# One order for three queues: the first stage and the last two pairs of a modulated 4-bit feed-forward kernel

## What is computed

```
gate = relu(cond @ W3 + b3)                                   # 64 x 512, one row per batch
v    = (64 * x + sum of x over the 64 positions) * gate       # x is 64 x 64 x 512
x1   = relu(v @ W2 + b2)                                      # the first stage
w_up = ((w_up_q - 7.5) * scale).T ;  w_down likewise          # 4-bit codes, a scale per 64
x2   = relu(x1 @ w_up + b_up + x1 @ up_a @ up_b)              # 512 -> 2048, low rank 16
out  = x + x2 @ w_down + b_down + x2 @ down_a @ down_b        # 2048 -> 512
```

## Time and profile before

| | us |
|---|---|
| median of 3 runs | 765.02 (764.61 to 765.81) |
| the profiled execution | 765.55 |
| its span in the profile | 763.7 |
| TensorE busy in the span | 740.0 (97%) |
| VectorE, ScalarE, GpSimd busy | 554.5, 420.4, 78.3 |

### The profile page before, as it was taken

How to read it: one execution, slowest core, us unless ns; L and a number is a source line. 1 busy time by engine, 2 the same in 40 slices (tenths; PEclk the granted TensorE clock), 3 DMA queues, 4 the chain that set the end, 5 groups by cost and what they waited for, 6 DMA issues and landing times. The chain is left out here.

```text
span 763.7 us, 9568 instructions
## 1 busy us (share of the span) xinstructions
PE 740.0 (97%) x3248; PEld 609.5 (80%) x3248; DVE 554.5 (73%) x725; ACT 420.4 (55%) x727; POOL 78.3 (10%) x68
## 2 busy tenths in 40 slices
PE   6599999999999999999999999999999999999997
PEld 5478888878878878888888888888888888888876
DVE  6598866776976487767776877767776877757585
ACT  3866175574754175666647265666656363626531
POOL 0063524333430000000000000000000000000000
PEclk9899999999999999999999999999999999999999
DMA  8957978988628696655516798766515696665552
GB/s 325 308 185 218 292 214 264 288 262 250 221 99 290 210 383 230 220 194 193 180 56 229 254 385 265 222 202 192 180 56 183 229 382 220 199 192 194 193 165 111
DMA packets 92160, 170.60 MB, mean 223 GB/s; under 512 B 8528, under 2 KB 25040, under 8 KB 91472
## 3 DMA queue, kind: packets, MB, share of 16 engines
q1 hardware_dynamic: 91824, 169.90, 67.4%
q10 hardware_dynamic: 288, 0.08, 0.0%
HBM read 130.10 MB, written 40.89 MB: 224 GB/s over the span
## 5 line engine op out<-in xcount | busy, mean ns | idle before, releaser
L1138 PE MATMUL ps<-x_hi,ring 128*128 128x512 f32 x672 | 262.1, 390 | 3.0 <-DVE x_lo L932 1.8
L1139 PE MATMUL ps<-x_lo,ring 128*128 128x512 f32 x672 | 261.5, 389 | 0.0
L1140 PE MATMUL ps<-x_hi,ring 128*128 128x512 f32 x672 | 261.4, 389 | 0.0
L1138 PEld LDWEIGHTS ps<-x_hi,ring 128*128 128x128 f32 x672 | 126.1, 188 | 31.4 <-DVE x_lo L932 2.7
L1140 PEld LDWEIGHTS ps<-x_hi,ring 128*128 128x128 f32 x672 | 126.1, 188 | 26.3
L1139 PEld LDWEIGHTS ps<-x_lo,ring 128*128 128x128 f32 x672 | 126.1, 188 | 26.1
L388 ACT ACTIVATE xt<-xt,gated,gate_n 128x64 f32<-128x64 f32 x216 | 74.6, 430 | 37.2 <-DVE gated L741 37.2
L497 ACT ACTIVATE f<-ps,bias 128x512 f32<-128x512 f32 x96 | 64.8, 690 | 42.2 <-PE ps L1140 42.2
L932 DVE TENSOR_TENSOR x_lo<-x_sum,x_hi 128x512 fp32r<-128x512 f32 x96 | 76.8, 818 | 4.2 <-ACT x_hi L535 3.4
L853 DVE TENSOR_TENSOR ps<-s,ps 128x512 f32<-128x512 f32 x48 | 33.3, 693 | 51.1 <-PE ps L1140 50.7
L890 DVE TENSOR_TENSOR res<-ps,res 128x512 f32<-128x512 f32 x72 | 48.3, 687 | 23.6 <-PE ps L1140 23.2
(11 more groups left out here) (80 smaller groups left out, 1002.0 us busy)
## 6 DMA issues: line engine op xcount, KB each, us to landing
ring<-made_w SPq DMA_DIRECT2D x336, 256.0 KB, 3.7
made_w<-made SPq DMA_DIRECT2D x16, 1280.0 KB, 6.0
xt<-in_x SPq DMA_DIRECT2D x32, 256.0 KB, 5.6
code<-in_codes SPq DMA_DIRECT2D x16, 512.0 KB, 8.3
scale<-made_s SPq DMA_DIRECT2D x16, 512.0 KB, 8.0
res<-in_x SPq DMA_DIRECT2D x4, 2048.0 KB, 10.1
made_w<-plain SPq DMA_DIRECT2D x64, 128.0 KB, 6.3
out<-res SPq DMA_DIRECT2D x12, 512.0 KB, 5.5
```

What stands on the lines that cost most here:

```text
L1138: pe.matmul(dest, w_hi, a_hi, start=start, stop=False, skip_group_check=True)
L1139: pe.matmul(dest, w_hi, a_lo, start=False, stop=False, skip_group_check=True)
L1140: return pe.matmul(dest, w_lo, a_hi, start=False, stop=stop, skip_group_check=True)
```

## The change

- TensorE, first stage: chunks 0 to 2 of half 0 run pass by pass (four matmuls high by high, four low weight by high, four high weight by low x), each pass with its own wait, so that the first four need only the high parts. `low_rank(0)` moves from behind tile 4 to behind tile 5.
- Who modulates: DVE tiles 0 and 2, ACT tiles 1, 4 and 7, POOL tiles 3, 5 and 6 (eight instructions of 64 columns each). POOL also rounds `lora` and `wide`; the tables are loaded on 96 of the 128 partitions, in two DMAs.
- Loads: `raw_w3` is sent by output chunk, the first quarter ahead; W2 goes over ACT's queue; the scales of the first two units are copied ahead of the others; x's tiles come in the order 0 to 5, 7, 6.
- DVE's and ACT's lists in the first stage are written in the order in which TensorE takes the tiles.
- Last block: the sums, roundings and subtractions of pairs 6 and 7 alternate, step by step. The very last `tail` is M6 before M7; M6 starts its bank afresh without waiting for a copy, ACT copies BP to `s4` beside it, and DVE adds `s4` to `res`.

The rest of the diff, cut to what is spoken of:

```diff
-    ON_DVE, ON_ACT = (0, 1, 2, 3, 5), (4, 6, 7)
+    ON_DVE, ON_POOL, ON_ACT = (0, 2), (3, 5, 6), (1, 4, 7)
...
             act.dma_start(raw_cond[:], cond[:]).then_inc(cond_loaded, 16)
+            for k in range(KD):
+                act.dma_start(raw_w2[:, k, :], w2[:, k, :]).then_inc(w2_raw[k], 16)
...
+            gate_tile(0)
             w2_high(0)
-            for k in range(KD):
             x_high(0, 0)
-            w2_high(1)
+            for k in range(1, KD):
+                gate_tile(k)
             act.wait_ge(gate_done, KD)
             act.mul(gate_n[:], gate[:], float(SEQ)).then_inc(gate_done, 1)
+            w2_high(1)
+            x_modulate(0, 1)
             x_high(0, 1)
...
+            def x_modulate(t):
+                pool.wait_ge(x_gated, gate_no(0, t))
+                pool.wait_ge(gate_done, KD + 1)
+                for b in range(PER):
+                    part = xt[:, j, k, b * SEQ:(b + 1) * SEQ]
+                    done = pool.tensor_scalar(part, part, gate_n[:, k, batch:batch + 1], gated[:, t, b:b + 1], ALU.mult, ALU.add)
+                done.then_inc(x_mod_pool, 1)
+
+            x_modulate(3)
+            pool.wait_ge(tables_loaded, 16)
+            pool.tensor_copy(lora_flat, raw_lora).then_inc(tab_cast, 1)
+            x_modulate(5)
+            x_modulate(6)
+            pool.tensor_copy(wide_flat[:, 0:T], raw_wide[:, 0:T]).then_inc(tab_cast, 1)
+            pool.wait_ge(rest_loaded, 16)
+            pool.tensor_copy(wide_flat[:, T:], raw_wide[:, T:]).then_inc(tab_cast, 1)
...
             w_tiles:
+                if s == 0 and j == 0 and k < KD - 1:
+                    passes = ((x_hi_done, w2_cast, w2_in_ring[k][:, 0], xm_hi[:, k, :]),
+                              (x_hi_done, w2_split, w2_in_ring[k][:, 1], xm_hi[:, k, :]),
+                              (x_split, w2_split, w2_in_ring[k][:, 0], xt_lo[:, j, k, :]))
...
+                if m == 1:
+                    pe.wait_ge(w3_loaded, 16)
...
-                    if j == 1 and k in (0, KD - 1):
-                        low_rank(k // 3)
+                    if j == 1 and k in (1, KD - 1):
+                        low_rank(k // 2)
...
             behind x_low of tile 7, DVE:
             add_lora(0)
-            x_low(0, 5)
             x1p_low(0, 0)
             x1p_low(0, 2)
-            x_low(0, 6)
+            plain_low(0)
             dequantize(1)
-            x_low(0, 7)
-            plain_low(0)
...
-            wide_low(slice(T, NH * P), 3)
             add_lora(1)
             x1p_low(1, 0)
             x1p_low(1, 2)
+            wide_low(slice(T, NH * P), 3)
...
-            tail(*before)
+            n = len(LAST) - 1
+            wait_bank(pe, BQ, SBS - 1, n)
+            product(SBS - 1, n, M6, BQ, True)
+            pe.wait_ge(q_down_done, down_no(SBS - 1, 3, 1) - 8 + 1)
+            product(SBS - 1, n, M7, BP, False)
```

More of the change, by code:

```diff
@@ L282, in load_scale, with copy_scales @@
                 sp.dma_start(scale[u % 3][:], rows.to_broadcast([2 * COPIES, P // 2 // COPIES, 1024])).then_inc(scale_loaded[u % 3], 16)
+            def copy_scales(units, copied):
+                n = units.stop - units.start
+                sp.dma_start(made_s[units], scales[units].unsqueeze(2).to_broadcast([n, 2, COPIES, 1024])).then_inc(copied, 16)
             def store_plain(u):
@@ L632, in _ @@
                     if n == 13 and last:
-                        x2_high(s, 6, 3)
+                        x2_high(s, 6, 2)
+                        x2_high(s, 7, 2)
+                    if n == 14 and last:
                         x2_high(s, 6, 4)
-                    if n == 14 and last:
-                        x2_high(s, 7, 3)
                         x2_high(s, 7, 4)
@@ L686, in _ @@
                         x2_high(s, (n - 1) // 2, 4)
-                    if n == 12 and last:
-                        x2_high(s, 6, 2)
-                    if n == 13 and last:
-                        x2_high(s, 7, 2)
                     if not last and n in (8, 10):
@@ L1131, in _ @@
             finish_c22(SBS - 1, 1)
+            to = res[:, 3, 1, :]
+            dve.wait_ge(q_down_done, down_no(SBS - 1, 3, 1) - 8 + 1)
+            dve.wait_ge(res_summed, 4 * (SBS - 2) + 4)
+            dve.tensor_tensor(to, to, s4[:], ALU.add).then_inc(res_summed, 1)
+            dve.wait_ge(res_summed, 4 * (SBS - 2) + 5)
+            add_res(*before, BQ)
             add_res(*before, BP)
-            add_res(*before, BQ)
         @block.tensor
@@ L1142, in w_tiles @@
             def w_tiles(s, j, k, bank_of):
+                if s == 0 and j == 0 and k < KD - 1:
+                    passes = ((x_hi_done, w2_cast, w2_in_ring[k][:, 0], xm_hi[:, k, :]),
+                              (x_hi_done, w2_split, w2_in_ring[k][:, 1], xm_hi[:, k, :]),
+                              (x_split, w2_split, w2_in_ring[k][:, 0], xt_lo[:, j, k, :]))
+                    for n, (x_ready, w_ready, still, moving) in enumerate(passes):
+                        pe.wait_ge(x_ready, k + 1)
+                        pe.wait_ge(w_ready, k + 1)
+                        for m in range(KD):
+                            mm = pe.matmul(ps[bank_of(m)][:], still[:, m * P:(m + 1) * P], moving, start=k == 0 and n == 0,
+                                           stop=False, skip_group_check=True)
+                    mm.then_inc(w_step, 1)
+                    return
                 pe.wait_ge(x_split, 8 * s + 4 * j + k + 1)
@@ L1334 @@
         "cond": tiles(a["cond_1024"].T),
-        "w3": tiles(a["cond_W3"]),
+        "w3": tiles(a["cond_W3"]).reshape(P, -1, kd, P).transpose(0, 2, 1, 3),
         "w2": tiles(a["cond_W2"]),
@@ L1339 @@
         "scales": scales,
-        "tables": np.concatenate([by_quadrant(a["ffn_w_up_lora_a"].T, 0), by_quadrant(a["ffn_w_down_lora_b"], rank), wide], 1),
+        "tables": np.concatenate([by_quadrant(a["ffn_w_up_lora_a"].T, 0), by_quadrant(a["ffn_w_down_lora_b"], rank), wide], 1)[:3 * QUAD],
     }
```

170 lines of the change are left out of this document (92 added, 78 removed).

## The result

| | before | after |
|---|---|---|
| median, us | 764.86 (764.61 to 765.81, 4 runs) | 755.45 (754.59 to 755.87, 4 runs) |
| span of the profiled execution | 763.7 | 753.9 |
| ratio | | 0.987, 95% interval 0.9856 to 0.989 |

The change takes 9.4 us off. I had forecast 748.7, 16.3 off, in a range of 744.5 to 756.0: the sign and the range hold, but the likeliest time was 6.8 too low, and 755.45 lies outside the 745 to 752 that I gave the forecast itself. The rest of this document is about those 6.8 us.

What follows compares the result with a forecast made beforehand. TensorE's pace bounds the kernel, with removable waits only in the first stage and last block. Gains of 13.5 - 0.5 + 3.3 = 16.3 us off the median 765.02 give 748.7; 8-in-10 range 744.5 to 756.

Steps and rivals of the forecast that it cites:

- POOL's price: First stage: each POOL instruction of 64 columns takes 0.5 us, bounds 0.19 to 1.3.
- rivals 1 and 2: First stage, POOL's instructions: 1.3 us each makes it the bound, 772 us, chance 0.04; 0.8 each, 758 us, chance 0.12.
- PE's waits at the tiles: First stage: 1.5 us of waits charged in all (0 to 4), with the low-rank group waiting 0.8.
- The low clock in the first tile: First stage: 10 of the first tile's 12 matmuls slower by 0.2 us each, 2.1 us charged (1.0 to 3.2).
- first tile: Start of the first stage: tile matmuls begin at 9.75 us (8.2 to 10.4) in place of 10.90.
- first tile to where `plain_unit(0)` could begin: First stage from 9.75: 21.8 + 1.0 work, 2.1 clock, 1.5 waits, so plain_unit(0) at 36.1 us.
- the hand-over: First stage into unit 0: add_lora(1) behind dequantize(1) uses up a 1.2 us cover; 0.5 us charged (0 to 2).
- block 0 behind unit 0: Units of block 0 after unit 0: no loss charged in the forecast, 0 us.
- last block: Last block: reordered pairs 6 and 7 and the replaced copy remove PE's stops, 3.3 us off (2.0 to 3.4).
- SP's queue: Load of res delays the stores behind it by some 8 us; not needed until unit 2, so nothing charged.
- Rival 3: Block 0: weights' loads, sums and stores come late and units 1 to 3 wait, about 5 us: 754, chance 0.14.
- My late bound: Start of the first stage: W3's rest lands by 7.6 us if ACT's queue moves as much; 7.0 taken.

Runs made afterwards that it cites:

- g1: Changed kernel with the edits of f1 and e2 plus, on SP, store_plain(u) ahead of the scales, codes and res; 749.50 us, ratio 0.979.
- d1: Changed kernel with dequantize(0) moved on DVE ahead of the low part of wide's first 512 columns; 756.12 us, ratio 0.988.
- w3: Changed kernel with the biases ahead of W2 on ACT's queue and W2's chunks 1 to 3 issued only after they landed; 756.04 us.
- p1: Changed kernel with one more wait: POOL holds off after wide's first 512 columns until DVE has finished plain_low(0); 754.97 us, ratio 0.986.
- d1p1: Changed kernel with both the edits of d1 and p1; 755.86 us, ratio 0.988.
- f1: Changed kernel with POOL's unit 0 sums after all four x1p_low, ACT rounding the rest of wide, x1p_low(1, *) around add_lora(1) before b_c22; 759.45 us.
- r1: Changed kernel with SP's load of res, and its wait, put behind store_plain(0) instead of ahead; 754.61 us, ratio 0.9861.
- f1r1: Kernel f1 with SP's load of res put behind store_plain(0); 753.34 us, ratio 0.9843.
- e2: Changed kernel with made_high(u) put on ACT ahead of the modulation of block 1's tile, units 4 to 11; 753.20 us, ratio 0.9838.
- g3: g1 with W3's rest heading ACT's queue behind cond, then biases, then W2; SP begins with W3's first rows and x's tiles; 748.50 us.
- g2: g1 with W3's rest ahead of x's tile 0 on SP and the biases ahead of W2 on ACT's queue; 750.16 us, ratio 0.9799.

## Why the prediction was right, and where its sum was off

**Right: what bounds, and where the stops go.** The 10.9 us of waits went with the new order, and tile 4 no longer waits behind the sums of tiles 7 and 6; no run takes DVE's order and the new loads apart. POOL's price, on which rivals 1 and 2 rest, is settled by the trace: eight instructions of 64 columns took 4.99 us for tile 3 and sixteen 8.49 for tiles 5 and 6, so 0.53 to 0.62 each against the 0.5 that I took. PE's waits at the tiles are 0.8 + 0.5 + 0.2 = 1.5, the sum that I charged, but by luck: I had the low-rank group wait 0.8 and tile 1 on time by 0.3, and it was tile 1 that waited 0.8 (15.66) and the group 0.2. The low clock in the first tile cost 1.25 (13.79 - 10.72 = 3.07 for eight matmuls of 0.227) instead of 2.1.

**The terms, measured against the forecast** (us that TensorE loses more, or less, than I had said):

| step | forecast | measured | off by |
|---|---|---|---|
| first tile | at 9.75 | 10.72 | +0.97 |
| first tile to where `plain_unit(0)` could begin | 26.35 | 27.4 | +1.1 |
| the hand-over | 0.5 | 4.0 | +3.5 |
| block 0 behind unit 0 | 0 | 1.5 | +1.5 |
| last block | -3.3 | -3.5 | -0.2 |

They add up to 6.9, about the 6.8. (The traces differ by 9.8, as the one of before has the stop of 0.5 in block 1; the medians by 9.4.) The 4.0 is 47.82 in the changed kernel against 43.76 for the same group in g1, which began its unit at 38.16. The 27.4 is 38.16 - 10.72, with the group's end as in g1; of it 21.8 + 1.0 are work, 1.5 waits and 1.25 low clock, and the other 1.9 are many small delays of 0.1 to 0.3 at the tiles' and groups' first matmuls, for which I had no term and which I didn't try apart. The clock's being 0.85 cheaper than charged hides half of them. The 1.5 of block 0 is of this one trace; by d1 and w3 it would be 0.1 to 0.2.

**The step that failed most** is the hand-over: charged 0.5 (0 to 2), it cost 4.0. I followed DVE's chain for x1's second half alone, with a cover of 1.2 us counted from when TensorE would begin the unit, and never for its own beginning: `add_lora(0)`, two `x1p_low`, `plain_low(0)`, behind a table that comes from POOL's queue. The rows were there: DVE's 3.99 beside POOL and the 3.46 of the earlier trace rows told that these steps cost 1.4 to 1.65 times as much next to POOL's sums (two take 2.42 alone). In the kernel before they lay beside tiles that were late themselves; with the tiles early this cover was gone. d1, p1 and d1p1 show that one can't win by half: the chain to `x1p_low(1, *)` sets it. f1 shows that it is won when POOL is kept out until that point, ACT rounds the table's rest and DVE takes `x1p_low(1, *)` ahead; the three weren't tried apart.

**The rule on the two engines.** The trace shows it as I cited it ("SBUF — State Buffer", "Who interferes with whom", in the Trainium skill): the same `dequantize(0)` took 2.49 us beside POOL and 1.22 without it. I used it for POOL's small instructions, where it cost almost nothing, and not for the place where both engines work on 1024 columns.

**SP's queue.** "Nobody needs these before unit 2, 23 us on, so nothing" gave the wrong reason: unit 2's `plain_high` stands in ACT's queue ahead of the rest of unit 1's tiles. In the changed kernel the 4.5 us that ACT waits there stop TensorE nowhere at once, and r1 doesn't show that they cost anything later. With the hand-over mended they do: in f1 the store was awaited until 9.3 us after its last issue (52.34 to 61.66) and TensorE stopped for 5.9, and f1r1 wins that back.

**Rival 3** (gain given back in block 0) happened for 1.5 us in the trace, not 5, and for another reason; the room that I had left for it and for rival 2 is why 755.45 still lies in the range. I had argued with bytes; e2 shows that an ACT order on which DVE waits makes the stops. They were there before: one stop of 0.78 stands in the trace of before at 170.67, and block 0 behind unit 0 took 1.2 us more there than in e2. I didn't ask what it would do if TensorE came earlier.

**The start.** My late bound, 7.6, was passed (8.14). It rested on the bytes ahead at the rate of before; w3 shows that W2's chunks 1 to 3 were not the cause. By the rule that I set beside it ("DMA: Bandwidth & Descriptors", "Issuing engines are not separate DMA queues", in the Trainium skill) a second issuer saves only issue time. In g3 W3's rest and tile 0 had both landed by 5.9, while on one queue the second of them came at 8.14 to 9.27, which is more than issue time (0.4 us a load). But g3 also puts W2's first chunk behind both, so it doesn't show whether the second issuer or the order brought it.

**With the mends.** g1 and g3 take 749.5 and 748.5, about what I had forecast for the change itself; what the prediction overlooked was to be had, but not with the change as it stood.

## What to carry to other kernels

When a change makes one stage earlier, cost the next hand-over anew from its first instruction, on every engine that feeds it: the lateness that goes was the cover of what stands behind. Where two engines slow each other, a stop that is mended by moving one of them comes back at the next thing they both owe, so look for the last such point and free the way up to there. And a store is not free because its data are needed late: look at who waits for its buffer, at what stands in that engine's queue behind, and at the bytes that go out ahead of it. When a run wins a microsecond in one stretch of one trace, look at that stretch in the other runs that leave it alone before you credit the edit.

## What the runs showed of the hardware

- DVE's 128x2 instruction took 0.16 us alone (f1) and 2.72 beside POOL's rounding of the 96x1536 table and the sum behind it (p1); POOL's sums of 256 columns 0.73 to 0.75 alone and 1.70 beside DVE. In these rows what a small DVE instruction lost went by POOL's instruction and not by its own size: it ended with POOL's, at 41.93 against 41.91 in p1, and the `x_gate` of 143.52 in the changed kernel at 144.79 against 144.76.
- TensorE stopped for 1.22 us in d1 and 1.21 in d1p1, at the first low-rank group, and 16 to 36 us kept a granted clock of 1.00. Stops of 1.88 (d1), 2.75 (changed) and 5.93 (f1) were each followed by a stretch at the lower level, 1.2 GHz: 0.50 granted in 42 to 44 us in d1, and in f1 eleven steps of 0.43 from start to start (67.53 to 72.22).
- A load's place in its queue went with some 3 us of its landing: W3's rest came at 5.18 ahead of tile 0 (g2, which also sends the biases ahead of W2) and at 8.44 behind it (g1), tile 0 at 8.68 and 5.95.
- A store that went out right behind a load of 2048 KB on the same queue had its buffer free 9.3 us after the last issue (f1); ahead of that load, within 3.4 us (f1r1, 51.47 to 54.88).
